# The last node update of a graph network: two DVE operations move behind the last attended evacuation, one variance moves one step later

## What is computed

```python
def _layer_norm(x, g, b, eps=1e-05):
    m = jnp.mean(x, axis=-1, keepdims=True)
    v = jnp.mean((x - m) ** 2, axis=-1, keepdims=True)
    return (x - m) * jax.lax.rsqrt(v + eps) * g + b
...
    agg = agg @ Wo + bo
    ...
    x = _layer_norm(node_embeddings + agg, ln1_g, ln1_b)
    h = jax.nn.gelu(x @ W1 + b1, approximate=False) @ W2 + b2
    return _layer_norm(x + h, ln2_g, ln2_b)
...
h = jnp.maximum(_layernorm(x, axis=-1), 0.0)
x = x + _L2_gnn_ref(h, edge_index, edge_type_8, ...)
h = jnp.maximum(_layernorm(x, axis=-1), 0.0)
x = x + _L3_gnn_ref(h, src, dst, edge_weight, L3_gnn_t)
return x
```

## Time and profile before

| | us |
|---|---|
| median of 3 runs | 4822.12 |
| lowest, highest | 4820.42, 4827.02 |
| the profiled execution | 4793.24 |
| its span | 4791.4 |
| first gather of this stage starts | 2762.32 |
| last gather of this stage ends | 3370.73 |
| last operation of this stage (`X` + `H` of tile 13) ends | 3480.02 |

### The profile page before, as it was taken

One profiled execution on the slowest core, in us unless ns is written; L12 is line 12 of the kernel. 1 busy time (PEld: TensorE's weight loads), 2 busy tenths in 40 slices (PEclk: granted clock), 3 DMA queues, 4 the chain that ended last, 5 costly groups with the idle time before them and its releaser, 6 DMA issues. The chain is left out here.

```text
span 4791.4 us, 53751 instructions
## 1 busy us (share of the span) xinstructions
PE 3037.5 (63%) x12326; PEld 1838.8 (38%) x12326; DVE 2708.5 (57%) x6253; ACT 916.2 (19%) x1645; POOL 2762.8 (58%) x2438
## 2 busy tenths in 40 slices
PE   3564745655797899664777657777646665555424
PEld 1222534544665687441222224545312222222113
DVE  7997742222457444675777727777745554444323
ACT  0332410000122000221222214334212221111100
POOL 0673057777111673446777678888157776877631
PEclk8876655555767555555555568787578887677655
DMA  6333621111455111542222244444111121333215
GB/s 255 79 71 121 268 82 24 24 24 23 114 158 152 34 26 25 177 177 87 41 41 43 35 72 91 107 87 105 65 45 36 37 38 30 32 28 30 24 14 109
DMA packets 337039, 363.11 MB, mean 76 GB/s; under 512 B 236961, under 2 KB 268843, under 8 KB 336864
## 3 DMA queue, kind: packets, MB, share of 16 engines
q1 hardware_dynamic: 219890, 261.52, 16.7%
q0 software_dynamic: 94096, 80.65, 13.9%
q10 hardware_dynamic: 22878, 18.95, 1.2%
HBM read 174.93 MB, written 201.00 MB: 78 GB/s over the span
## 5 line engine op out<-in xcount | busy, mean ns | idle before, releaser
L801 PE MATMUL e_ps<-e_msg,e_hot 128*128 x2408 | 571.4, 424 | 222.9 <-issue 213.0
L801 PEld LDWEIGHTS e_ps<-e_msg,e_hot 128*128 128x128 f32 x2408 | 530.1, 329 | 301.8 <-issue 301.8
L1767 POOL DMA_INDIRECT u_a<-attended,dst_end x392 | 489.3, 1248 | 149.9 <-issue 119.1
L2401 PE MATMUL d_pl<-d_hot,d_fields 128*65 128x512 f32 x712 | 479.8, 836 | 0.0
L774 DVE TENSOR_TENSOR sums<-e_ps,sums 128x455 f32 (+1 forms) x172 | 108.1, 628 | 557.2 <-PE e_ps L801 557.2
L719 POOL DMA_INDIRECT e_msg<-from_src,e_src x200 | 192.5, 962 | 286.2 <-DMA e_first<-lot_first 227.2
L2345 POOL DMA_INDIRECT flows<-d_out,d_end x160 | 263.6, 1648 | 107.1 <-issue 104.7
L1424 ACT ACTIVATE u_zt<-u_pt 128x256 f32<-128x256 f32 (+1 forms) x392 | 164.2, 433 | 840.4 <-PE u_pt L1319 838.8
L2056 POOL DMA_INDIRECT list<-s_rec,s_place x200 | 200.6, 1003 | 212.5 <-DVE s_place L1972 156.5
L2332 POOL DMA_INDIRECT d_near<-term,d_rec x196 | 191.0, 975 | 194.3 <-DMA d_rec<-list 135.1
L724 POOL DMA_INDIRECT e_msg<-h1d,e_src x200 | 204.9, 1025 | 120.3 <-issue 60.6
(11 more groups left out here) (383 smaller groups left out, 7249.3 us busy)
## 6 DMA issues: line engine op xcount, KB each, us to landing
x<-sums SPq DMA_DIRECT2D x28, 896.0 KB, 7.8
u_x<-x SPq DMA_DIRECT2D x28, 896.0 KB, 5.7
terms<-s_zeros SPq DMA_DIRECT2D x16, 812.5 KB
s_key_row<-src_key SPq DMA_DIRECT2D x50, 256.0 KB
term<-u_h SPq DMA_DIRECT2D x14, 910.0 KB, 3.7
flows<-s_zeros SPq DMA_DIRECT2D x14, 896.0 KB
n_x<-in_x SPq DMA_DIRECT2D x14, 896.0 KB
h<-n_h SPq DMA_DIRECT2D x14, 896.0 KB
```

The lines of the kernel that those rows point to most:

```text
L801: last = nc.tensor.matmul(to, hot[s][:, q, :], rows, start=False, stop=q == LOT - 1)
L1767: pool.indirect_dma_start(A[s][:, j, :], None, net.attended[:, :], bass.IndirectOffsetOnAxis(ap=net.dst_end[:, tile:tile + 1], axis=0)).th ...
L2401: last = nc.tensor.matmul(pl[0:WEIGHT + 1, :], fields[:, j, :], hot[:, j, :], start=j == 0, stop=j == J - 1)
```

## The change

In `attend` of DVE the product and the sum leave their places after evacuations 3 and 4, with the drain in front of each, and are written after the last evacuation, behind the signal `inputs_used`, with one drain behind both. In `mlp` the variance of the new `X` is written after evacuation 6 instead of 5. Instructions, tiles and semaphores stay the same.

```diff
-                            if t is not None and i == 3:
-                                v.drain()
-                                nc.vector.tensor_tensor(TG[t[1]][:, :, :], T[t[1]][:, :, :], channels(net.norms[:, 0, :]), ALU.mult)
-                            if x is not None and i == 4:
-                                v.drain()
-                                nc.vector.tensor_tensor(X[x[1]][:, :, :], X[x[1]][:, :, :], H[x[1]][:, :, 0:C], ALU.add).then_inc(tail_ready, 1)
                         v.drain()
                         if c is not None:
                             v.sem_inc(inputs_used, 1)
+                        if t is not None:
+                            nc.vector.tensor_tensor(TG[t[1]][:, :, :], T[t[1]][:, :, :], channels(net.norms[:, 0, :]), ALU.mult)
+                        if x is not None:
+                            nc.vector.tensor_tensor(X[x[1]][:, :, :], X[x[1]][:, :, :], H[x[1]][:, :, 0:C], ALU.add).then_inc(tail_ready, 1)
+                        v.drain()
...
                                 elif i == 4:
                                     centre(xs, 1)
-                                elif i == 5:
+                                elif i == 6:
                                     variance(2 * y[0] + 1, 1)
```

## The result

| | before | changed |
|---|---|---|
| median of 4 runs each | 4823.32 us | 4792.78 us |
| lowest, highest | 4820.42, 4827.02 | 4789.32, 4800.25 |
| the profiled execution | 4793.24 | 4800.25 |

The ratio is 0.9938 (95% interval 0.9921 to 0.9956): the change makes the kernel about 30 us faster. I had forecast no difference, 4822 us, and the range ended at 4815. And yet the two traces agree with the forecast: in them the changed kernel is not faster at all. One of the 84 plain runs of the kernel before that stand beside the experiments took 5073.13 us, in a slower state of the chip, and is left out everywhere.

The account below looks back on a forecast made before the run. POOL's 392 gathers, plus what is left after the last one, were taken to bound the last node update. Last gather -3.4 us and tail +3.0 us gave -0.4 us: 4822 us, range 4815 to 4830.

Parts of the forecast that it names:

- PE becomes the bound: Rival, chance 0.06: the change widens PE's pause between MLP and next attention, MLPs stay at clock 0.50, 4835 us.
- (3) (b): Tail, ACT's copies for MLP 13: variance starts 3.78 us after the centring instead of 6.15, -2.37 us.
- (1) and (2), the gathers: Loop of the last node update: two steps take 90.0 us instead of 90.8, the last gather ends 3.4 us earlier.
- The price of the later variance: Variance behind the MLP's last evacuation: loop operations 0.5 to 0.83 us later, +1.93 us twice in the tail.
- the shift: H, T and centring operations 0.5 us later in six steps, 0.83 in two; POOL's period follows one to one.
- (3) the tail: After the last gather DVE and ACT are the path: 1.93 - 2.37 + 1.93 + 1.53 = +3.0 us.
- (c): Tail, end of MLP 13: variance +1.93 us; then centring to next reciprocal 7.98 us instead of 6.45, +1.5.
- Gathers freed for good: Rival, chance 0.03: in the loop, product and sum hold no gather in their new place, -28 + 3 us, 4797 us.
- The clock back in the last MLP: Rival, chance 0.05: PE's pause before tile 13's MLP shrinks to 3.7 us, high clock returns, -5.5 us, 4816 us.
- Sum: Whole last node update: gathers -3.4 us plus tail +3.0 us, -0.4 us in all.
- hand count of the holds: POOL's gathers in a step: any gather beginning inside a big DVE operation ends 0.82 us after that operation.

Follow-up runs that it names:

- e2_again: The changed kernel run once more without an edit: 4800.36 us, ratio 0.9960 to the kernel before.
- e3_behind: The changed kernel with the variance of the new X back at its old place, product and sum still moved: 4787.18 us, ratio 0.9932 to the kernel before.
- e11_behind: e3_behind run once more without an edit: 4781.83 us, ratio 0.9914 to the kernel before.
- e1_same: The kernel before run once more without an edit: 4819.95 us, ratio 0.9996.
- e4_late_var: The kernel before with only the variance of the new X moved, after evacuation 6 instead of 5: 4829.25 us, ratio 1.0017.
- e12_swap_nofill: The kernel before with Y's variance after evacuation 4, the sum after 5, and no unread matmuls ahead of the MLP's first product: 4821.12 us, ratio 1.0002.
- e9_fill10: The kernel before with 10 instead of 4 unread matmuls ahead of the MLP's first product: 4811.35 us, ratio 0.9966.
- e8_product: The kernel before with only the product moved behind the last attended evacuation: 4803.48 us, ratio 0.9955.

## Why the prediction was wrong

**The step that failed** stands in the first lines: the plain runs have a median "about 29 us more, and I carry any difference over to them unchanged". The traced execution lay 27 us under the lowest of the plain runs, which themselves lay within 6.6 us. I took that for a constant that profiling or the chip adds. It was the effect itself: the trace showed an execution in which PE keeps up with POOL, and the usual one is another, in which it falls behind. "POOL never waits for anybody. So this stage lasts as long as its 392 gathers, 28 for each of 14 tiles, plus what is left to do after the last one" held in both kinds (608.4 and 608.7 us to the last gather); what was left to do was 109 us in one and 135 in the other.

**The rival was the right mechanism on the wrong kernel.** *PE becomes the bound*, with an MLP at 0.50 that costs 5.5 us and PE falling behind step by step, was given 0.06, as something that the change might bring on. It was the state of the kernel before, and the change took it away. The row that I used against it, PE's 4.5 us to spare in the earlier trace rows, is of the execution that had them. What I had not looked at is DVE's order in the attention from a lagging PE's side: that the product and the sum stand ahead of a variance for which ACT's root waits, and ACT's copies for the MLP behind that. I looked at this queue in the tail only, as (3) (b), where the trace showed it.

**What was forecast inside the trace, where PE keeps up, point by point:**

- *(1) and (2), the gathers.* Two steps were to take 90.0 us together; from 3063.50 to 3153.57 they took 90.1, and steps 7 to 12 were 45.0 to 45.6 each. The last gather came 2.2 us earlier, in e2_again 2.1, forecast 3.4. The scaling of `H` started 37.1 us and the centring 42.2 us into tile 8, forecast 36.8 and 41.9: ACT's copy came 3.07 us behind the MLP's last evacuation (3139.34 to 3142.41), forecast 2.65.
- *The price of the later variance.* Without the shift the last gather was to end 7.4 us earlier; in e3_behind it was 8.8 and in e11_behind 10.9. In the runs the variance costs 13 us, and the terms that I had for it, 4.0 in the gathers and 1.93 twice in the tail, make 7.9. This term was too small; in the traces it is 11.5 (719.2 to 707.7), 6.6 of it in the gathers. What makes it larger in the gathers no run shows by itself; the last section has a candidate.
- *(3) the tail.* +3.0 was forecast, +3.6 and +3.0 measured. Centre to variance in (b) 3.79 us, forecast 3.78; from centring to reciprocal in (c) 8.02, forecast 7.98.
- *The rivals.* Gathers freed for good: no, both holds hit, on the gathers that begin 7.80 and 10.21 us into the tile, forecast 7.80 and 10.22. The clock back in the last MLP: no, that MLP took 24.98 us again (3433.20 to 3458.18), though PE's pause ahead of it was 3.73 us in place of 6.09.
- *Sum.* Stage +1.5 us in the first trace of the changed kernel and +0.9 in the second, forecast -0.4.

So the working inside the trace was good to two us, and the answer was wrong by thirty, since it was made for an execution that the kernel before rarely runs.

**What stays open.** I can't say what makes a given MLP slow. Over the 180 MLPs of the fifteen traces in the table, by the time that PE paused for ACT's copies in the 5 us ahead of the MLP's first product (added up where there were two such pauses):

| pause | MLPs | slow |
|---|---|---|
| none, or up to 0.42 us | 117 | 6 |
| 0.54 to 1.43 us | 36 | 17 |
| 1.64 us and more | 27 | 26 |

All six of the first row are in kernels without the four unread matmuls. The middle row goes either way: after 0.54 us, the MLP of tile 7 of e1_same was fast and that of tile 8 slow.

The pause is not the only thing that comes with the lag. The windows of the end of an attention show another, first in the first trace of before, where PE waits for gathers, then in e1_same, where it lags:

```profile
3098.00:3107.00 9.00, 7.07 (x24) 3.99 (x24) 4.16 (x4) 2.72 (x5) 7.02 (x7) 0.50 0.75 221
```

```profile
3110.00:3118.00 8.00, 4.71 (x28) 2.94 (x27) 7.76 (x8) 2.67 (x5) 6.78 (x5) 1.00 0.29 98
```

Where PE keeps up, the granted clock is at 0.50 there and rises at the MLP: in all 111 fast MLPs of the table's first row it rose between 1.3 us before the first product and 2.0 us after it. Where PE lags, the clock has often risen in the attention already: 5.7 to 13.5 us ahead of the product in the eight slow MLPs of e1_same and e4_late_var whose pause was 2.3 to 2.6 us, and it fell within 1.7 us after the product. Whether the pause ends such a stretch or it would have ended anyway, no experiment separates. The early rise alone is not enough: behind one of 6.3 us or more stood six fast MLPs of e12_swap_nofill, three of e9_fill10 and one of e8_product. It isn't settled either why the kernel before sometimes gets through, as in its first trace. And what an execution does up to tile 5, where the first slow MLPs come and POOL's first steps are only 35 to 43 us, would need several traces of the same kernel.

## What to carry to other kernels

Before a trace is used to forecast, hold its own time and clock against the plain runs: if it lies outside them, the trace shows another course of the kernel, and the difference is not to be carried over. Where an engine follows another at a small distance, ask what the loop looks like once it has fallen behind, which waits then vanish and which appear, and whether a lagging step is longer than a leading one. And the operation on which another engine's whole queue waits (here variance, root, copies, MLP) goes ahead of those that nobody waits for.

## What the runs showed of the hardware

**PE stays at the low clock through busy work.** In e1_same PE was busy for 24.18 of the 25.00 us of an MLP and the granted clock was 0.50 throughout, while at the high clock the same MLP keeps PE busy 14.00 of 19.00 us, as the window of the kernel before's first trace shows:

```profile
3110.00:3129.00 19.00, 14.00 (x88) 9.38 (x88) 16.49 (x14) 8.83 (x16) 15.34 (x13) 0.88 0.68 122
```

The Trainium skill (TensorE: Matmul & The Clock Gate, What's actually happening) says that the gate follows how busy PE has lately been; the traces agree in that the longer pauses ahead were followed by the low clock (26 of 27 of 1.64 us and more), and that of e1_same shows no return while the work of this MLP went on.

**A gather and a DVE operation that begin together.** DVE and POOL in e1_same, twice, each pair within 0.07 us:

```profile
3103.26 2.06 DVE L1537 SCALAR_TENSOR_TENSOR u_h<-u_xc,u_rstd 128x1792 f32<-128x1792 f32 x1
...
3282.74 2.02 DVE L1524 SCALAR_TENSOR_TENSOR u_xc<-u_mean,u_x 128x1792 f32<-128x1792 f32 x1
```

```profile
3103.27 0.95 POOL L1767 DMA_INDIRECT u_a<-attended,dst_end  x1 [0.30 <-issue]
...
3282.81 2.77 POOL L1767 DMA_INDIRECT u_a<-attended,dst_end  x1 [0.30 <-issue]
```

When the gather starts 0.01 us after the operation, it takes 0.95 us, and DVE 2.06 in place of 2.02. When it starts 0.07 us after, it takes 2.77 and DVE is not touched. In the fifteen traces, all 197 gathers that started within 0.02 us of such an operation, before or after it, took 0.94 or 0.95 us, and all 111 that started 0.05 to 0.30 us after it took 2.55 to 2.79. The 125 that started 0.05 to 0.30 us before it took 0.94 or 0.95 us too, and left DVE its 2.02 or 2.03. My hand count of the holds treated both alike. So a shift of DVE by a few hundredths decides over 1.8 us on POOL, which may be part of what the later variance cost beyond my estimate; that was not tried. The Trainium skill (SBUF — State Buffer, Who interferes with whom) says for contention over the shared ports that the order of issue decides who blocks; here the traces agree for the gather, which waits when the operation is clearly first, but a gather that begins first, or within 0.02 us, lengthens the operation by 0.06 us at most, and not by its whole 0.95.
